# Third feed-forward: second weights centred ahead, squares summed on ScalarE, the up product in three fp32r parts and the bias rows on TensorE

## The chip, the cores and the metric

The kernel runs on one core of one Trainium2 chip. The time is the device time of one execution in microseconds (us). Three runs of the kernel before gave 1136.63, 1144.24 and 1147.08 us (median 1144.24).

The core has a matrix engine (TensorE, PE in the rows, its weight loads PEld), a vector engine (VectorE, DVE), a scalar engine (ScalarE, ACT), a general engine (GpSimd, POOL) and a queue that issues transfers (SyncE, SP).

## The reference, cut to what matters

Eight blocks run one after the other on 2048 tokens of 128 features (attention and feed-forward, four times), each as `x = x + block(layernorm(x))`. The change is in the sixth, the third feed-forward, with eight experts:

```python
def _L2_ffn_ref(x, gate_w, w1, w2, b1, b2, ln_g, ln_b):        # E = 8, D = 128, hidden 256
    scores = xt @ gate_w
    ew, ei = top_k(scores, 2); ew = softmax(ew)
    wE = sum(ew[None] * mask, axis=-1)                          # weight of expert e for token t
    h = gelu(einsum('td,edf->etf', xt, w1) + b1[:, None])
    o = einsum('etf,efd->etd', h, w2) + b2[:, None]
    z = xt[None] + o
    y = (z - mean(z)) * rsqrt(var(z) + 1e-6) * ln_g + ln_b      # over D, for every expert and token
    return einsum('et,etd->td', wE, y)
```

All eight experts are computed for all tokens; the weights of the six that a token does not use are zero. `xt` is itself a layer-normed x, so its mean over D is zero up to rounding.

## The kernel before

Each block is a function that adds instructions to five engine queues; `program` calls them in order, so every engine runs its part of block 5, then of block 6, and so on. Nothing but semaphores ties the queues together. `Norm` normalises x at the start of a block: VectorE writes `xn` (tokens on partitions), TensorE transposes it in four chunks of 512 tokens (`NC` = 4, `CH` = 512, `TPC` = 4 tiles of 128), ScalarE copies each chunk into `xnT`. If a block asks for it (`split_xnT`), ScalarE then also writes each chunk rounded to fp32r (`x_high`), GpSimd the rest of it (`x_low`), and TensorE's `wait_xnT` waits for the second too.

`l2_ffn` (L1309) runs 32 steps, eight experts times four chunks. What a step consists of, engine by engine:

- TensorE: `up` (L1377), two products of 128 x 128 weights with 512 columns in fp32, into two of four banks; `down` of the step before (L1389), eight fp32 products of 128 columns into a bank of its own. One fp32 product stands in the trace as two records.
- ScalarE: two Gelus (L1443) on the results of `up`, into `hT`; then `zn` of three steps before (L1435), four scalings of z by 1/sigma with a shift.
- VectorE: `sums` (L1529) z = result of `down` + (xn + b2); four `bn_stats` (L1533); `shift` of the step before (L1550), -mean/sigma; four `bn_aggr` (L1540) and the variance plus eps (L1543); `add` of three steps before (L1560), four times x += z * weight.
- GpSimd: 1/sigma by a power (L1477); xn + b2 for two steps on (L1466); z * ln_g of two steps before (L1470).
- SyncE: the weights of expert e, 257 KB with b1, into one of two slots (L1339).

The first eight steps are written out, then the engines run a loop over pairs of experts. Ahead of step 0 TensorE computes the router's logits (L1367); it waits until VectorE has copied them (`step`, L1508) before the first `up`. ScalarE takes the router's Exp (L1426) before its first Gelu. In step 0 and 1 the router weights are transposed (L1401) and multiplied with ln_b (L1409), and VectorE adds the four results to x (L1567), in the midst of its first steps.

The next block (`l3_attn`) starts its normalisation on VectorE inside the last steps (`after`, L94 and L98) and has 32 records of TensorE work (L1660) that needs nothing of x.

## Time and profile before

| what | value |
|---|---|
| runs | 1136.63, 1144.24, 1147.08 us |
| profiled execution | 1135.98 us, of which 1134.2 us span |
| busy over the span | PE 917.4 us (81%), DVE 677.8 (60%), POOL 550.0 (48%), ACT 433.0 (38%) |
| mean granted TensorE clock | 0.888 of 2.4 GHz |
| from the first `up` of the block (639.72 us) to the end of the next block's last statistics (796.53 us) | 156.8 us |

In these tables "busy" is the time in which an engine executes; a gap in it costs something only if the engine decides the pace at that place. Rows of the timeline read: start in us, duration in us, engine, line of the kernel, operation, what it writes and reads with partitions x elements, and how many equal ones were merged; in brackets how long the engine had been idle before and what ended that. Groups of instructions read: line, engine, operation, shapes, count, then total busy us and mean ns of one. The granted clock is 1.00 at 2.4 GHz and 0.50 at 1.2 GHz.

### The profile page before, as it was taken

The numbers are of one execution on the slowest core, as the hardware profiler recorded it, in microseconds if no ns is written. First come the engines' busy times: TensorE is split into PE (matmuls) and PEld (weight loads), VectorE is DVE, ScalarE is ACT, GpSimd is POOL, SyncE is SP. The second block draws the span as 40 slices with busy tenths as digits, with TensorE's granted clock in tenths as the row PEclk, the third lists the DMA queues.
The fourth block names the chain that finished last, engine by engine and source line by source line (L and its number), as shares of the span: only waits on it lengthen the run. The fifth ranks groups of instructions, "written<-read, shape, count | busy, mean of one in ns | idle before, by whom it ended". The sixth has DMA issues, their size and how long they took to land. (4 is left out here: it accounts for less than half of the span.)

```text
span 1134.2 us, 18018 instructions
## 1 busy us (share of the span) xinstructions
PE 917.4 (81%) x6494; PEld 592.5 (52%) x6494; DVE 677.8 (60%) x1706; ACT 433.0 (38%) x876; POOL 550.0 (48%) x430
## 2 busy tenths in 40 slices
PE   4559999999989878267999899994699997299993
PEld 2113333333333446164566676663697667199883
DVE  6756667767660255979677479999302475643334
ACT  2334665566555422014111356665344211032221
POOL 4335977897788611152312158888300001146661
PEclk9658999999997988658799699998799998599997
DMA  5700111011000000001000000030200000166665
GB/s 169 222 1 2 29 30 30 2 29 30 3 1 23 1 21 8 9 6 56 2 1 2 1 10 20 19 128 0 75 1 1 1 10 29 55 191 214 211 206 143
DMA packets 37815, 56.40 MB, mean 50 GB/s; under 512 B 5643, under 2 KB 25091, under 8 KB 37607
## 3 DMA queue, kind: packets, MB, share of 16 engines
q1 hardware_dynamic: 35238, 50.21, 14.5%
q0 software_dynamic: 2496, 5.12, 1.6%
q8 instruction: 51, 0.84, 0.3%
q14 instruction: 30, 0.24, 0.1%
HBM read 44.17 MB, written 10.94 MB: 49 GB/s over the span
## 5 line engine op out<-in xcount | busy, mean ns | idle before, releaser
L671 DVE TENSOR_REDUCE arena<-ps 128x2 f32<-128x1024 f32 (+2 forms) x192 | 177.3, 955 | 86.9 <-PE ps L487 55.5
L420 POOL TENSOR_TENSOR arena<-arena 128x1024 f32<-128x1024 f32 (+3 forms) x105 | 201.3, 1957 | 38.8 <-ACT arena L606 38.8
L606 ACT ACTIVATE arena<-ps 128x512 f32<-128x512 f32 (+3 forms) x320 | 138.8, 489 | 91.4 <-PE ps L519 57.6
L117 POOL TENSOR_SCALAR vareps<-meanvar 128x4 f32<-128x4 f32 x32 | 7.8, 245 | 234.6 <-DVE meanvar L98 234.6
L511 PE MATMUL ps<-arena 51*128 51x512 bf16 (+3 forms) x384 | 91.4, 345 | 18.0 <-ACT arena L606 6.8
L152 PE MATMUL ps<-ident,xn 128*128 128x128 f32 x128 | 27.2, 365 | 69.2 <-DVE xn L106 25.4
L511 PEld LDWEIGHTS ps<-arena 51*128 51x128 bf16 x384 | 26.9, 94 | 106.9 <-ACT arena L606 59.7
L2058 PE MATMUL ps<-arena 128*128 128x128 f32 x624 | 78.1, 279 | 0.0
L1389 PEld LDWEIGHTS ps<-arena 128*128 128x128 f32 x512 | 60.8, 192 | 30.7 <-ACT arena L1443 20.3
L2058 PEld LDWEIGHTS ps<-arena 128*128 128x128 f32 x624 | 74.6, 196 | 0.0
L420 POOL TENSOR_TENSOR xnT<-xnT,arena 128x1024 f32<-128x1024 f32 (+1 forms) x28 | 52.8, 1907 | 42.1 <-ACT xnT L606 42.1
L1389 PE MATMUL ps<-arena 128*128 128x128 f32 x512 | 64.6, 279 | 8.4 <-ACT arena L1443 8.4
L487 PE MATMUL ps<-arena 48*128 48x512 bf16 (+3 forms) x320 | 56.1, 346 | 17.5 <-DVE arena L671 14.8
L540 PE MATMUL ps<-arena 128*9 128x512 f32 (+3 forms) x640 | 68.2, 502 | 0.0
L1435 ACT ACTIVATE arena<-arena 128x128 f32<-128x128 f32 x128 | 52.7, 482 | 38.7 <-DVE arena L1550 38.7
L1377 PE MATMUL ps<-xnT,arena 128*128 128x512 f32 x128 | 64.6, 631 | 0.4 <-DVE arena L1508 0.4
L165 ACT ACTIVATE xnT<-ps 128x512 f32<-128x512 f32 x32 | 18.9, 596 | 113.0 <-PE ps L152 106.1
L2224 DVE TENSOR_TENSOR arena<-ps,arena 128x512 f32<-128x512 f32 x39 | 27.0, 691 | 58.5 <-PE ps L2058 57.7
L2018 POOL DMA_INDIRECT expert_rows<-arena x39 | 38.5, 988 | 42.7 <-ACT arena L2106 42.1
L152 PEld LDWEIGHTS ps<-ident,xn 128*128 128x128 f32 x128 | 20.7, 191 | 72.9 <-issue 48.1
L1477 POOL TENSOR_TENSOR arena<-arena,power 128x4 f32<-128x4 f32 x32 | 34.6, 1081 | 46.5 <-DVE arena L1543 46.5
L2005 POOL DMA_INDIRECT arena<-token_rows,arena x39 | 38.0, 974 | 39.0 <-DVEq L2206 27.1
(319 smaller groups left out, 1985.7 us busy)
## 6 DMA issues: line engine op xcount, KB each, us to landing
arena<-in_L_ffn_w SPq DMA_DIRECT2D x39, 512.0 KB, 4.2
arena<-scratch SPq DMA_DIRECT2D x32, 192.0 KB, 3.9
scratch<-arena SPq DMA_DIRECT2D x12, 256.0 KB, 3.9
arena<-in_L_ffn_w SPq DMA_DIRECT2D x8, 257.0 KB, 2.7
arena<-in_L_ffn_w SPq DMA_DIRECT2D x8, 256.0 KB, 4.0
arena<-expert_rows SPq DMA_DIRECT2D x8, 256.0 KB, 4.8
scratch<-arena SPq DMA_DIRECT2D x4, 384.0 KB, 5.1
scratch<-arena SPq DMA_DIRECT2D x12, 128.0 KB, 4.2
```

Of the source, the lines that this page charges most:

```text
L152: last = nc.tensor.transpose(m.ps[:, self.banks[n % len(self.banks)], j * P:(j + 1) * P], m.xn[:, n * TPC + j, :], m.ident[:, :])
L420: nc.gpsimd.tensor_tensor(e, e, weight[:, at:at + k].unsqueeze(1).broadcast_to([P, 2, k]), ALU.mult).then_inc(weighed, 1)
L487: mm = nc.tensor.matmul(m.ps[:, bank + e, 0:wd], qs[rows, u % BUFS, pair, at * P:(at + 1) * P], ks[rows, u % BUFS, pair, j:j + wd], start= ...
L511: mm = nc.tensor.matmul(m.ps[:, bank, 0:wd], ks[rows, u % BUFS, p, kt * P:(kt + 1) * P], qs[rows, u % BUFS, p, CH * qc:CH * qc + wd], star ...
L540: mm = nc.tensor.matmul(m.ps[PAD * h:PAD * h + HD + 1, 7, 0:wd], vones[:, b * TB + kt, u % G * GH + h, :], probs(u * NG + n)[:, h, 0:wd], ...
L606: nc.scalar.activation(probs(g)[:, 2 * p + e, 0:wd], m.ps[:, BANK[h, e], 0:wd], ACT.Exp, scale=SCALE).then_inc(exps, 1)
L671: nc.vector.tensor_reduce(out, scores, AX.X, ALU.max, negate=True).then_inc(max_set, 1)
L1377: mm = nc.tensor.matmul(m.ps[:, 2 * (k % 2) + f, :], w[:, u, W1 + f * P:W1 + (f + 1) * P], m.xnT[:, c * CH:(c + 1) * CH], start=True, stop ...
L1389: mm = nc.tensor.matmul(m.ps[:, 4 + k % 2, j * P:(j + 1) * P], hT[:, k % 2, f, j * P:(j + 1) * P], w[:, u, W2 + f * P:W2 + (f + 1) * P], s ...
L1435: ins = nc.scalar.activation(z[:, k % 4, j, :], z[:, k % 4, j, :], ACT.Identity, bias=nb[:, k % 4, j:j + 1], scale=rs[:, k % 4, j:j + 1])
L2018: nc.gpsimd.indirect_dma_start(m.expert_rows, bass.IndirectOffsetOnAxis(ap=target_i[:, s:s + 1], axis=0), y[:, s % RING, :], None,).then_i ...
L2058: mm = nc.tensor.matmul(m.ps[:, 2 * (s % 2) + half, f * P:(f + 1) * P], w_up[:, s % WBUFS, at + f * P:at + (f + 1) * P], xgT[:, s % 2, :], ...
```

## The change

What it does, in the function `l2_ffn` alone:

- The mean over D is taken out beforehand: w2 has its row means subtracted (`w2_mean` on VectorE, `w2c` on GpSimd, once for each expert), b2 its mean (once). z then has mean zero, so `shift`, `bn_stats` and `bn_aggr` fall away, and so does `zn`. The variance is the mean of z squared: four Square activations with an accumulated output (`squares`) on ScalarE.
- GpSimd computes mean square / D + eps, the power, and its product with the router weight (three small instructions). Its two 128 x 512 instructions in a step fall away.
- b2 enters by TensorE: one fp32r product per step (`pick` selects the two rows, high and low part, of the expert), the first of each `down`.
- `up` becomes three fp32r products for each of its two halves (high x high, high x low, low x high). For that `split_xnT` is asked for, ScalarE rounds w1 (`w1_high`), GpSimd takes the rest (`w1_low`), once for each expert, one expert ahead.
- VectorE: `sums` adds xn directly; `add`, now of two steps before, is y = z * (weight/sigma) * ln_g in four instructions and then x += y in one.
- Order: the first `up` no longer waits for the copied logits; the Exp, the six instructions on the router weights, the transposes and the ln_b products are moved into steps 1, 4, 5 and 6. Loops become written-out steps. z has three buffers instead of four.
- Transfers: b1 for all experts at once, b2 as 2 x 8 rows instead of 512 KB, w without b1 (256 KB), its slots released by the conversions and no longer by `down`.

The diff, cut:

```diff
+    m.rounded.fresh()
+    x_high, x_low = norm.split_xnT()
 ...
+        for e in range(E):
+            if e >= 2:
+                sp.wait_ge(w1_low_set, e - 1)
+                sp.wait_ge(w2_centred, e - 1)
+            sp.dma_start(w[:, e % 2, :], A["L2_ffn_w"][e, :, 0:2 * F]).then_inc(w_in[e % 2], 16)
 ...
+        def up(n):
 ...
+            if n >= 2:
+                pe.wait_ge(h_done, FT * (n - 1))
             for f in range(FT):
-                mm = nc.tensor.matmul(m.ps[:, 2 * (k % 2) + f, :], w[:, u, W1 + f * P:W1 + (f + 1) * P], m.xnT[:, c * CH:(c + 1) * CH],
-                                      start=True, stop=True)
-                mm.then_inc(up_done, 1)
+                nc.tensor.matmul(out, w1_high[:, e % 2, fs], x_high[:, cs], start=True, stop=False)
+                nc.tensor.matmul(out, w1_high[:, e % 2, fs], x_low[:, cs], start=False, stop=False)
+                nc.tensor.matmul(out, w1_low[:, e % 2, fs], x_high[:, cs], start=False, stop=True).then_inc(up_done, 1)
+        def down(n):
 ...
+            if n >= 2:
+                pe.wait_ge(z_done, n - 1)
+            nc.tensor.matmul(m.ps[:, 4 + n % 2, :], pick[:, e, :], b2_rows[:, :].unsqueeze(1).broadcast_to([P, TPC, D]), start=True, stop=False,
+                             skip_group_check=True)
             for f in range(FT):
+                pe.wait_ge(h_done, FT * n + f + 1)
 ...
-        pe.wait_ge(step, 1)
+        for n in range(STEPS):
+            up(n)
+            if n:
+                down(n - 1)
+            if n == 4:
+                turn_weights()
+            if n == 6:
+                norm_biases()
+        down(STEPS - 1)
 ...
+        def squares(n):
+            act.wait_ge(z_done, n + 1)
 ...
+            for j in range(TPC):
+                ins = nc.scalar.activation(square[:, j, :], z[:, n % 3, j, :], ACT.Square, accum_out=ss[:, n % 4, j:j + 1])
 ...
+            if n == 1:
+                act.wait_ge(step, 2 + RANK_STEPS)
+                nc.scalar.activation(gap[:, :], gap[:, :], ACT.Exp).then_inc(exps, 1)
+            if n == 4:
+                for c in range(NC):
+                    turn(c)
+            if n:
+                squares(n - 1)
+            if c == 1 and e + 1 < E:
+                round_weights(e + 1)
 ...
+            nc.gpsimd.tensor_scalar(ve[:, n % 4, :], ss[:, n % 4, :], 1.0 / D, EPS, ALU.mult, ALU.add).then_inc(scales, 1)
+            nc.gpsimd.tensor_tensor(rs[:, n % 4, :], ve[:, n % 4, :], m.power[:, 0:TPC], ALU.pow).then_inc(scales, 1)
+            nc.gpsimd.tensor_tensor(wrs[:, n % 4, :], rs[:, n % 4, :], wte[:, c * TPC:(c + 1) * TPC, e], ALU.mult).then_inc(scales, 1)
+            if c == 1 and e + 1 < E:
+                split_weights(e + 1)
 ...
+        def add(n):
+            e, c = divmod(n, NC)
+            dve.wait_ge(scales, 3 * n + 3)
 ...
             for j in range(TPC):
-                ins = nc.vector.bn_stats(st[:, k % 4, j, :], z[:, k % 4, j, :])
+                ins = nc.vector.scalar_tensor_tensor(out=y[:, j, :], in0=z[:, n % 3, j, :], scalar=wrs[:, n % 4, j:j + 1], in1=lng[:, e, :],
+                                                     op0=ALU.mult, op1=ALU.mult)
 ...
+            nc.vector.tensor_tensor(xs, y[:, :, :], xs, ALU.add).then_inc(y_done, 1)
```

In the lists below a row is one instruction in the order of its engine's queue, or several equal ones in a row (x4); one fp32 matmul is one row here.

VectorE, one step in the midst of the block. Before (L1529 is `sums`, L1533 `bn_stats`, L1550 `shift`, L1540 and L1543 the variance, L1560 `add`):

```order
L1529 TENSOR_TENSOR arena<-ps,arena 128x512
L1533 BN_STATS arena<-arena 128x6 x4
L1550 SCALAR_TENSOR_TENSOR arena<-arena 128x4
L1540 BN_AGGR arena<-arena 128x2 x4
L1543 TENSOR_SCALAR arena<-arena 128x4
L1560 SCALAR_TENSOR_TENSOR x<-arena,x 128x128 x4
```

And of the changed kernel (L1571 is `sums`, L1580 and L1585 are `add`, L1520 and L1522 the mean of w2, once in four steps):

```order
L1571 TENSOR_TENSOR arena<-ps,xn 128x512 [waits l2f_o_done,l2f_y_set]
L1580 SCALAR_TENSOR_TENSOR arena<-arena 128x128 [waits l2f_y_done,l2f_scales]
L1580 SCALAR_TENSOR_TENSOR arena<-arena 128x128 x3
L1585 TENSOR_TENSOR x<-arena,x 128x512 [waits l2f_y_set]
L1520 TENSOR_REDUCE arena<-arena 128x2 [waits l2f_w2_centred,l2f_w_in1]
L1522 TENSOR_SCALAR arena<-arena 128x2 [waits l2f_w2_summed]
```

Of 15 instructions in a step six are left; nothing between `sums` and `add` waits for GpSimd's work on the same step or the one before.

ScalarE, from the last chunk of xnT to step 3, of the changed kernel (L1466 Gelu, L1469 the Exp, L1453 the squares, L1440 the rounding of w1):

```order
L168 ACTIVATE rounded<-xnT 128x512
L1466 ACT_TABLE_LOAD
L1466 ACTIVATE arena<-ps,arena 128x512 x4
L1469 ACT_TABLE_LOAD
L1469 ACTIVATE arena<-arena 128x16
L1453 ACTIVATE arena<-arena 128x128 x4
L1440 ACTIVATE rounded<-arena 128x256
L1466 ACT_TABLE_LOAD
L1466 ACTIVATE arena<-ps,arena 128x512 x2
L1453 ACTIVATE arena<-arena 128x128 x4
```

Before, the same place held one table load:

```order
L165 ACTIVATE xnT<-ps 128x512 x4
L1426 ACTIVATE arena<-arena 128x16
L1443 ACT_TABLE_LOAD
L1443 ACTIVATE arena<-ps,arena 128x512 x4
L1429 ACTIVATE arena<-ps 8x512 x4
```

The Exp has moved behind four Gelus, and the tables are loaded three times in place of once; after that no step loads any.

TensorE, steps 4 and 5 of the changed kernel (L1384 to L1386 are the three parts of `up`, L1397 the bias, L1402 `down`):

```order
L1397 MATMUL ps<-rounded 128x512 [waits l2f_z_done,l2f_w2_centred]
L1402 MATMUL ps<-arena 128x128 [waits l2f_h_done]
L1402 MATMUL ps<-arena 128x128 x3
L1402 MATMUL ps<-arena 128x128 [waits l2f_h_done]
L1402 MATMUL ps<-arena 128x128 x3
L1384 MATMUL ps<-rounded 128x512 [waits l2f_h_done]
L1385 MATMUL ps<-rounded 128x512
L1386 MATMUL ps<-rounded 128x512
```

Where a step had two matmuls of 512 columns and eight of 128, all fp32, it has seven of 512 columns in fp32r and the same eight.

## Rows read from the trace of the kernel before

**Rows 1.** Window, steps 10 to 31: stretch; PE, PEld, DVE, ACT, POOL busy (count); clock; DMA; GB/s.

```profile
697.00:778.00 81.00, 72.79 (x400) 48.89 (x400) 74.41 (x300) 54.77 (x119) 68.76 (x60) 1.00 0.16 55
```

**Rows 2.** Timeline, VectorE, one step and the start of the next.

```profile
749.52 0.69 DVE L1529 TENSOR_TENSOR arena<-ps,arena 128x512 f32<-128x512 f32 x1 [0.19 <-DVE x L1560]
...
750.25 0.87 DVE L1533 BATCH_NORM_STATS2 arena<-arena 128x6 f32<-128x128 f32 x4
...
751.16 0.67 DVE L1550 SCALAR_TENSOR_TENSOR arena<-arena 128x4 f32<-128x4 f32 x1
751.75 0.37 DVE L1540 BATCH_NORM_AGGREGATE arena<-arena 128x2 f32<-128x6 f32 x4
...
752.15 0.17 DVE L1543 TENSOR_SCALAR arena<-arena 128x4 f32<-128x4 f32 x1
752.34 1.14 DVE L1560 SCALAR_TENSOR_TENSOR x<-arena,x 128x128 f32<-128x128 f32 x4
...
753.67 0.69 DVE L1529 TENSOR_TENSOR arena<-ps,arena 128x512 f32<-128x512 f32 x1 [0.19 <-DVE x L1560]
```

**Rows 3.** Timeline, ScalarE and GpSimd, the same step.

```profile
750.54 1.26 POOL L1470 TENSOR_TENSOR arena<-arena 128x512 f32<-128x512 f32 x1
...
751.86 1.65 ACT L1435 ACTIVATE arena<-arena 128x128 f32<-128x128 f32 x4 [1.35 <-DVE arena L1550]
...
752.40 1.17 POOL L1477 TENSOR_TENSOR arena<-arena,power 128x4 f32<-128x4 f32 x1 [0.59 <-DVE arena L1543]
...
753.42 1.24 ACT L1443 ACTIVATE arena<-ps,arena 128x512 f32<-128x512 f32 x2
```

**Rows 4.** Timeline, TensorE, an early step: `up`, `down`, the next `up`.

```profile
664.01 1.88 PE L1377 MATMUL ps<-xnT,arena 128*128 128x512 f32 x4
...
665.73 1.95 PE L1389 MATMUL ps<-arena 128*128 128x128 f32 x16
...
667.51 1.88 PE L1377 MATMUL ps<-xnT,arena 128*128 128x512 f32 x4
```

**Rows 5.** Timeline, TensorE, fp32r products of 512 columns in the next block.

```profile
811.52 0.39 PE L1669 MATMUL ps<-rounded 128*128 128x512 f32 x1
...
811.75 0.39 PE L1670 MATMUL ps<-rounded 128*128 128x512 f32 x1
```

**Rows 6.** Timeline, start of the block: first logits, their copy, `up` of steps 0 and 3.

```profile
630.92 1.81 PE L1367 MATMUL ps<-arena,xnT 128*128 128x8 f32 x8
...
639.38 0.29 DVE L1508 COPY arena<-ps 128x128 f32<-128x128 f32 x1 [7.38 <-PE ps L1367]
...
639.72 6.41 PE L1377 MATMUL ps<-xnT,arena 128*128 128x512 f32 x8 [0.38 <-DVE arena L1508]
...
660.51 1.88 PE L1377 MATMUL ps<-xnT,arena 128*128 128x512 f32 x4
```

**Rows 7.** Timeline, the next block splits a chunk of xnT.

```profile
802.42 0.63 ACT L168 ACTIVATE rounded<-xnT 128x512 fp32r<-128x512 f32 x1
...
803.12 1.40 POOL L125 TENSOR_TENSOR rounded<-xnT,rounded 128x512 fp32r<-128x512 f32 x1 [4.82 <-ACT rounded L168]
```

**Rows 8.** Window, `up` of steps 0 and 1; columns as in rows 1.

```profile
639.70:646.30 6.60, 6.41 (x8) 2.49 (x8) 4.83 (x18) 2.80 (x5) 0.00 (x0) 0.58 0.00 0
```

**Rows 9.** Timeline, ScalarE: the table load ahead of the first Gelu.

```profile
643.70 1.28 ACT L1443 ACT_TABLE_LOAD   x1
```

**Rows 10.** Groups by line and shape: a 128 x 128 Exp, small GpSimd instructions.

```profile
L117 POOL TENSOR_SCALAR vareps<-meanvar 128x4 f32<-128x4 f32 x32 | 7.8, 245 | 234.6 <-DVE meanvar L98 234.6
...
L2100 ACT ACTIVATE arena<-arena 128x128 f32<-128x128 f32 x1 | 0.3, 309 | 0.0
```

**Rows 11.** Timeline, the end: next block's first load, last `down`, last statistics.

```profile
745.24 0.34 SPq L1652 DMA_DIRECT2D arena<-in_L_attn_wqkT  x1
...
775.36 2.02 PE L1389 MATMUL ps<-arena 128*128 128x128 f32 x16 [2.18 <-ACT arena L1443]
...
796.15 0.38 DVE L98 BATCH_NORM_AGGREGATE meanvar<-stats 128x2 f32<-128x6 f32 x4
```

More of the change, by code:

```diff
@@ L1353, in pipelined @@
[L1353 to L1360 removed]
+        sp.dma_start(b1[:, :, :], A["L2_ffn_w"][:, :, B1:B1 + FT].rearrange("e p n -> p e n")).then_inc(small_in, 16)
+        for e in range(E):
[3 more added lines that the diff above has]
+            sp.dma_start(w[:, e % 2, :], A["L2_ffn_w"][e, :, 0:2 * F]).then_inc(w_in[e % 2], 16)
@@ L1376, in up @@
             for f in range(FT):
[L1377 to L1386 removed]
+                fs = slice(f * P, (f + 1) * P)
@@ L1567, in add_biases @@
             nc.vector.tensor_tensor(xs, m.ps[:, 6 + c % 2, :].rearrange("p (j d) -> p j d", d=D), xs, ALU.add).then_inc(lnb_added, 1)
-        def body(i, k, n):
-            sums(i, k, n)
-            if n == 0:
-                for c in range(NC):
-                    add_biases(c)
-                dve.wait_ge(lnb_added, NC)
-            if n is None or n >= 1:
-                shift(i, k - 1)
-            variance(i, k)
-            if n is None or n >= 3:
-                add(i, k - 3, None if n is None else n - 3)
-        def tail():
-            shift(E // 2 - 1, UNROLL - 1, last=True)
-            after(dve, 0)
-            for k in range(UNROLL - 3, UNROLL):
-                add(E // 2 - 1, k, None)
-                after(dve, k % NC)
-        pipelined(dve, body, tail)
-    total = E * NC
-    return Part([(y_done, total - NC + c + 1) for c in range(NC)], tensor=tensor, vector=vector, scalar=scalar, gpsimd=gpsimd, sync=sync,
+        for n in range(STEPS):
+            e, c = divmod(n, NC)
+            sums(n)
+            if n == 1:
+                weights()
+            if n >= 2:
+                add(n - 2)
+                if n - 2 >= STEPS - NC:
+                    after(dve, n - 2 - (STEPS - NC))
+            if n == 5:
+                dve.wait_ge(y_done, n - 1)
+                for k in range(NC):
+                    add_biases(k)
+                dve.wait_ge(lnb_added, NC)
+            if c == 1 and e + 1 < E:
+                sum_weights(e + 1)
+        for n in (STEPS - 2, STEPS - 1):
+            add(n)
+            after(dve, n - (STEPS - NC))
+    return Part([(y_done, STEPS - NC + c + 1) for c in range(NC)], tensor=tensor, vector=vector, scalar=scalar, gpsimd=gpsimd, sync=sync,
                 early=False)
```

267 lines of the change are left out of this document (126 added, 141 removed).

## The prediction

> **What bounds the kernel now.** I read the windows first, then the timeline of one step, then the two ends of the block. In the late part of the block, VectorE is busy for 74.4 of 81.0 us, TensorE for 72.8 and GpSimd for 68.8 [rows 1]; three engines near 90% say little by themselves, so the step decides. VectorE's starts of `sums` lie 4.15 us apart (749.52 and 753.67). Between them it has 0.69 for `sums`, 0.87 `bn_stats`, 0.67 `shift`, 0.37 and 0.17 for the variance, 1.14 `add`, sum 3.91, and 0.19 us of idling that ends with its own `add` [rows 2]. So it waits for no other engine: VectorE sets the pace. One item of it is inflated: `shift` handles 128 x 4 elements and yet takes 0.67 us; it ends at 751.83, when GpSimd's L1470 ends (750.54 + 1.26 = 751.80) [rows 2, 3]. ScalarE waits 1.35 us per step for VectorE and GpSimd 0.59 [rows 3]. TensorE alone is faster: in the early steps, while its lead lasts, `up` to `up` is 667.51 - 664.01 = 3.50 us without a gap, 1.72 for `up` and 1.78 for `down` [rows 4]. The whole block with its tail runs from 639.72 [rows 6] to 796.53 [rows 11].
>
> **TensorE's step after.** An fp32r product of 512 columns starts 0.23 us after the one before (811.52, 811.75) [rows 5]. `up` is six of them, 1.37 us in place of 1.72; `down` keeps 1.75 us (sixteen records, 0.11 each, [rows 4]) and gains one for the bias, 1.98. Sum 3.35 us. That the bias product reads the same 128 columns four times has no row; I take it as the others, and 32 of them at double the price would be 7 us.
>
> **VectorE's step after.** `sums` 0.69; four multiplications at the pace of L1560, 1.14; one sum over 128 x 512, taken as `sums`, 0.69; the mean of w2 once in four steps, at most 0.7, that is 0.17; hand-overs 0.15. Sum 2.85 us in place of 4.1: it is no longer the bound.
>
> **ScalarE's step after.** Two Gelus 1.24 [rows 3], the rounding of w1 at most 0.4 in four steps, 0.1, and four squares. No square with an accumulated output is in the trace. Bound from below: 0.31 us, what a 128 x 128 Exp takes [rows 10]. Above: `zn` has four of the same size in 1.65 us, 0.39 apart, and if the read of the accumulator counts as another 128 x 128 instruction, 0.39 + 0.31 = 0.70. I take 0.35, nearer the Exp, since a square has no per-partition scale and the read hands over one number for each partition. Sum 1.24 + 0.1 + 1.4 = 2.75 us, under TensorE's 3.35; at 0.50 us per square it would reach it.
>
> For the same operation the Trainium skill ("ScalarE: Activation LUTs", What ACT_TABLE_LOAD costs) gives 186 ns plus 0.83 ns per column, 93 ns for each pointer operand, and 93 ns overlap of neighbours. As an estimate from that page a square of 128 columns with one pointer comes to 0.29 us, without the read; the sum would be 2.5 us and the result the same, since TensorE decides.
>
> **GpSimd's step after.** 0.25 [rows 10], 1.06 to 1.17 for the power [rows 3], 0.25, and per expert one instruction of 128 x 256 and two of 128 x 128, each below the 1.26 us of 128 x 512 [rows 3], so under 0.95 per step. At most 2.6 us: hidden. Its chain square, power, weight is needed by `add` two steps later, 6.7 us, and takes about 2; hidden.
>
> **Waits in the loop.** `up(n)` waits for the Gelus of n-2, `down(n)` for the Gelus of n and for `sums(n-2)`. On ScalarE the squares of n-2 stand ahead of the Gelus of n. From the end of `down(n-2)` to `down(n)` TensorE has 1.37 + 1.98 + 1.37 = 4.7 us of work; `sums` 0.9, squares 1.4, Gelu 0.6 and three hand-overs of 0.2 need 3.5. Slack 1.2 us, so no wait is expected: the pace is 3.35 us.
>
> **The block as four stretches, before against after.**
>
> 1. *Start.* TensorE now waits for `x_low` of a chunk before its logits. Behind the transposes ScalarE needs 0.63 us more and GpSimd 1.40 [rows 7], with hand-overs 2.2 us for the first chunk (first logits at 630.92 [rows 6]), and about 1.3 more for the last, whose splitting is only partly hidden. `up(0)` at 643.2 in place of 639.72: **+3.5 us**. VectorE's preparation of the b2 rows and of w2's first mean, thirteen instructions, twelve of them at 0.3 like L1508 and one of 128 x 1024 at twice the 0.69 of 128 x 512, 5 us, lies in its 7.38 us of idling [rows 6].
> 2. *`up(0)` to `up(3)`.* Before 20.8 us (639.72 to 660.51 [rows 6]): transposes and ln_b products lie in it. After: three `up`, two `down`, 8.1 us at full clock; the granted clock was 0.58 in the first 6.6 us, mostly the level of 1.2 GHz [rows 8], and as much time at that level costs 3.3; the second table load and the Exp delay Gelu 2, with about 0.5 us left of it on TensorE. 11.9 us: **-8.9**.
> 3. *`up(3)` to the end of the last `down`* (before 775.36 + 2.02 = 777.38 [rows 11], 116.9 us). After 29 x 1.37 + 30 x 1.98 = 99.1; the transposes, sixteen at 0.11, 1.8 and 0.3 of waiting; the ln_b products, 32 records, 3.5, and 1.5 because their third group waits for VectorE, which adds the first only behind `add(3)`; 0.7 at the last Gelu. 106.9 us: **-10.0**.
> 4. *Tail to the end of the last statistics.* Before 796.53 - 777.38 = 19.2 us, since VectorE was more than one step late. After, VectorE has behind the last `down` `sums` 0.9, three `add` at 1.95 and three statistics at 1.27 (0.87 and 0.38 [rows 2, 11]), hand-overs 0.2 each and a wait for the last scale of some 1: 12.3 us: **-6.9**.
>
> Sum 3.5 - 8.9 - 10.0 - 6.9 = **-22.3 us**, that is 1136.0 - 22 = 1114 against the profiled execution's own time. The next block finds its weights: their transfers began at 745.24 [rows 11], behind the last expert's, and the new release of the slots (by the conversions, one expert earlier) brings them forward. So all that follows moves with it. The three runs before span 1136.6 to 1147.1 and the profiled one is at the lower edge; the middle of that span less 22 is **1119 us**, by the median it would be 1122.
>
> **Table loads.** The Exp's move costs two loads more, 1.28 us each [rows 9], ahead of Gelu 2; after it no step has one. The same page of the Trainium skill counts 2.66 us for a switch, with a drain of 1.38 that no row here shows; by it the two would delay Gelu 2 by 2.8 us more and the sum would be 19.5. The trace decides for the smaller figure: the row holds the 1.28 and no drain.
>
> **Rivals.**
>
> A. *ScalarE becomes the bound.* Above 0.50 us per square each further 0.1 costs 0.4 us per step. At 0.60, the middle of the upper half of my bounds, a step is 3.8 us and the gain falls to 10: 1131 us. For it: no row shows the read. Against it: an Exp with its write of 128 columns takes 0.31. 15%.
>
> B. *VectorE is blocked by GpSimd (slower).* `shift` stood still until L1470 was through [rows 2, 3]. The new `add` reads two SBUF tensors in all five instructions; if each of GpSimd's (some 2.1 us per step with the expert's share) held it up in full, VectorE would need 2.85 + 2.1 = 4.95 us. Thirty-two steps at 4.95 in place of 3.35 are 51 us more than forecast, of which some 10 us fall into waits that stretches 2 to 4 count already: 1119 + 41 = 1160 us. It decides from 1.2 us of blocking per step. Against it: `add` at 752.34 ran beside the power of 752.40 and took 1.14 us for four, no more than at any other place [rows 2, 3], and nearly all of GpSimd's time is now the power. 5%.
>
> The Trainium skill ("SBUF — State Buffer", the part on the shared port pair) says the same as B: a VectorE instruction with two SBUF inputs and a GpSimd instruction that reads SBUF exclude each other for the whole instruction. The stretched `shift` agrees, the unhindered `add` beside the power does not.
>
> C. *The moved pieces cost more than their length.* The router weights pass VectorE, ScalarE's Exp, GpSimd's first scale and TensorE's transposes, and each of them has steps queued behind it. If each hand-over stalls TensorE for a step's length of 3.35 us at two or three places, 8 us are lost: 1127 us. For it: VectorE stands in the ln_b additions, with `sums` behind them. Against: TensorE's lead over `sums` is two steps. 12%.
>
> D. *The fp32r parts run as fp32.* Then `up` is 6 x 0.85 = 5.1 us, a step 7.3 and the time far above 1200. The rows of the next block exclude it but for an unforeseen form [rows 5]. 1%.
>
> **How the numbers follow.** Forecast 65%; A 15, C 12, B 5, D 1, other 2. Range 1104 to 1134: below, the forecast from the lowest run (1136.6 - 22 = 1114.6) with shorter squares, no waits in stretches 2 and 3 and a tail without waiting (some 5 us) and 5 for the scatter of the runs; above, A and C with the same scatter. A difference under 1% (11 us) cannot be told from none here. Faster by over 1%: the forecast, C and two thirds of A, 87%; within 1%: the rest of A and the strong form of C, 7%; slower by over 1%: B and D, 6%.
>
> **What would show it.** Starts of `up` 3.35 us apart with no idle time on TensorE in the late part, at clock 1.00; VectorE some 2.85 us busy per step and waiting for TensorE's `down`; four squares in 1.3 to 1.5 us; `up(0)` 3.5 us later against the first statistics; from the last `down` to the last statistics 12 us. Wrong if squares take over 0.5 us apart, if instructions of `add` end when GpSimd's end, if TensorE waits for a Gelu in each step, or if L1397 takes over 0.25 us.

## The result, and the profile after

| | time, us (median; lowest to highest) | ratio to before, 95% interval |
|---|---|---|
| before | 1144.86 (1136.63 to 1148.09) | |
| after | 1134.14 (1127.27 to 1136.08) | 0.9906, 0.9889 to 0.9922 |
| forecast | 1119 (1104 to 1134) | |

The change gains 10.7 us (0.9%), less than half of what was forecast, and the time lies just outside the range, at its upper end. The profiled execution after spans 1127.3 us; before it was 1134.2.

For all comparisons below I use two marks in the traces, since they leave out the scatter of the other seven blocks: the first transpose of the block (L152) and the end of the last statistics of the next block (L98). Before, they are at 629.08 and 796.53 us, 167.5 us apart. After, 158.3 us apart, and 157.1 in a second profile of the same kernel. The block gained 9 to 10 us, nearly what the medians say (10.7); so nothing of it was given back in the last block. The two profiles of one kernel differ by 1.2 us, nearly all of it ahead of `up(2)`: from the first transpose to `up(2)` it is 21.2 us in one and 20.0 in the other, according to whether the granted clock falls 5 us ahead of the first transpose or only at it. The profiles of the experiments start in one of these two ways (the last two kernels change the start itself), so a difference of about 1 us counts only between two that start alike.

TensorE, the last step of expert 2 and the first of expert 3 after the change (L1384 to L1386 `up`, L1397 the bias product, L1402 `down`; columns as in the timelines of before):

```profile
692.31 0.48 PE L1384 MATMUL ps<-rounded 128*128 128x512 f32 x1
692.63 0.39 PE L1385 MATMUL ps<-rounded 128*128 128x512 f32 x1
...
693.77 0.40 PE L1397 MATMUL ps<-rounded 128*128 128x512 f32 x1
694.01 1.95 PE L1402 MATMUL ps<-arena 128*128 128x128 f32 x16
697.28 0.50 PE L1384 MATMUL ps<-rounded 128*128 128x512 f32 x1 [1.33 <-POOL rounded L1484]
...
700.71 0.48 PE L1384 MATMUL ps<-rounded 128*128 128x512 f32 x1
```

This answers to [rows 4]. Inside an expert `up` follows `up` after 3.40 us, as at 697.28 and 700.71, without a gap. But from the last step of one expert to the first of the next it takes 4.97 us (692.31 to 697.28): TensorE waits for L1484, GpSimd's part of the splitting of w1. An expert takes 15.20 us (697.28, 712.48, 727.68, 742.88, 758.08) where four steps are 13.6. The view of the waits of TensorE between 641 and 775 us (us in total, times, longest):

```profile
PE ps L1384 <- POOL rounded L1484: 8.5, 6, 1.9
PE ps L1422 <- DVE x L1590: 1.4, 1, 1.4
PE ps L1412 <- ACT arena L1458: 0.2, 1, 0.2
```

Why the split is late stands in two more timelines of the same stretch. ScalarE (L1440 rounds w1, L1453 the squares of step 9):

```profile
691.17 0.40 ACT L1440 ACTIVATE rounded<-arena 128x256 fp32r<-128x256 f32 x1
...
693.38 0.31 ACT L1453 ACTIVATE arena<-arena 128x128 f32<-128x128 f32 x1 [0.66 <-DVE arena L1571]
693.60 0.19 ACT L1453 ACTIVATION_READ_ACCUMULATOR arena<-arena 128x1 f32 x1
693.70 0.29 ACT L1453 ACTIVATE arena<-arena 128x128 f32<-128x128 f32 x1
```

GpSimd (L1498 to L1504 the three scale instructions of a step, L1484 the split, L1489 the centring of w2):

```profile
692.95 0.21 POOL L1504 TENSOR_TENSOR arena<-arena 128x4 f32<-128x4 f32 x1
694.83 0.35 POOL L1498 TENSOR_SCALAR arena<-arena 128x4 f32<-128x4 f32 x1 [1.67 <-ACT arena L1453]
695.26 1.01 POOL L1500 TENSOR_TENSOR arena<-arena,power 128x4 f32<-128x4 f32 x1
696.35 0.20 POOL L1504 TENSOR_TENSOR arena<-arena 128x4 f32<-128x4 f32 x1
696.50 0.73 POOL L1484 TENSOR_TENSOR rounded<-arena,rounded 128x256 fp32r<-128x256 f32 x1
697.21 1.28 POOL L1489 TENSOR_SCALAR arena<-arena 128x128 f32<-128x128 f32 x2
```

The rounded w1 of expert 3 is there at 691.57. GpSimd is free from 693.16 to 694.83, but the split stands in its queue behind the scales of step 9, and these wait for the squares of step 9, which end at 694.7. The split is over at 697.23; TensorE could have started at 695.7. "One expert ahead" in the code is, in time, not ahead at all: when GpSimd works on step 9, TensorE, which leads by two to three steps, is already at the end of step 11.

The second place is behind step 6, where the ln_b products now lie (L1422). Timeline of TensorE after the change, from the end of step 6 to `up` of step 8:

```profile
668.23 1.95 PE L1402 MATMUL ps<-arena 128*128 128x128 f32 x16
670.11 2.05 PE L1422 MATMUL ps<-arena 8*128 8x128 f32 x16
673.53 3.22 PE L1422 MATMUL ps<-arena 8*128 8x128 f32 x16 [1.38 <-DVE x L1590]
676.68 0.80 PE L1384 MATMUL ps<-rounded 128*128 128x512 f32 x1
677.28 0.63 PE L1385 MATMUL ps<-rounded 128*128 128x512 f32 x1
...
679.84 2.50 PE L1402 MATMUL ps<-arena 128*128 128x128 f32 x16
682.10 0.48 PE L1384 MATMUL ps<-rounded 128*128 128x512 f32 x1
```

And the window of the last 5.3 us of it (stretch; PE, PEld, DVE, ACT, POOL busy; clock; DMA; GB/s):

```profile
676.70:682.00 5.30, 5.30 (x23) 4.62 (x23) 1.28 (x3) 1.37 (x2) 1.20 (x2) 0.59 0.20 49
```

The forecast had the products and the wait, 5.0 us; they take 6.6 (670.11 to 676.68). It did not have the clock: in the second half of the products it falls to 1.2 GHz, the products take twice as long, and nearly all of the next step is slow too, 5.42 us in place of 3.40 (676.68 to 682.10).

### The profile page after: what moved, and what is told of

The parts are those of the page before. It is cut to its first block and busy times, and to the rows that moved or that the text cites. A ratio compares the mean times of both kernels' runs of the same rounds, so it can differ in the third digit from the quotient of the medians.

```text
span 1127.3 us, 17905 instructions
## 1 busy us (share of the span) xinstructions
PE 908.3 (81%) x6590; PEld 612.6 (54%) x6590; DVE 646.1 (57%) x1445; ACT 429.1 (38%) x1018; POOL 510.8 (45%) x458
## 5 line engine op out<-in xcount | busy, mean ns | idle before, releaser
L152 PE MATMUL ps<-ident,xn 128*128 128x128 f32 x128 | 26.4, 356 | 62.1 <-DVE x L922 19.9
L2076 PEld LDWEIGHTS ps<-arena 128*128 128x128 f32 x624 | 74.7, 196 | 0.0
L2242 DVE TENSOR_TENSOR arena<-ps,arena 128x512 f32<-128x512 f32 x39 | 27.0, 692 | 66.0 <-PE ps L2076 34.7
L1402 PEld LDWEIGHTS ps<-arena 128*128 128x128 f32 x512 | 63.0, 194 | 2.9
L1402 PE MATMUL ps<-arena 128*128 128x128 f32 x512 | 62.9, 276 | 0.0
L152 PEld LDWEIGHTS ps<-ident,xn 128*128 128x128 f32 x128 | 20.0, 186 | 66.0 <-issue 40.7
L1453 ACT ACTIVATE arena<-arena 128x128 f32<-128x128 f32 x128 | 38.0, 298 | 35.8 <-DVE arena L1571 35.8
L1267 DVE TENSOR_TENSOR arena<-ps,arena 128x512 f32<-128x512 f32 x64 | 39.7, 682 | 17.6 <-PE ps L1149 17.6
L2110 ACT ACTIVATE arena<-ps 128x512 f32<-128x512 f32 x39 | 23.3, 597 | 68.1 <-PE ps L2076 58.3
```

The source lines that it names most:

```text
L152: last = nc.tensor.transpose(m.ps[:, self.banks[n % len(self.banks)], j * P:(j + 1) * P], m.xn[:, n * TPC + j, :], m.ident[:, :])
L1267: nc.vector.tensor_tensor(at[:, t % 2, g, :].rearrange("p (j q) -> p j q", q=P), m.ps[:, g, :].rearrange("p (j q) -> p j q", q=P), causal[ ...
L1402: mm = nc.tensor.matmul(m.ps[:, 4 + n % 2, j * P:(j + 1) * P], hT[:, n % 2, f, j * P:(j + 1) * P], w2c[:, e % 2, f, :], start=False, stop= ...
L2076: mm = nc.tensor.matmul(m.ps[:, 2 * (s % 2) + half, f * P:(f + 1) * P], w_up[:, s % WBUFS, at + f * P:at + (f + 1) * P], xgT[:, s % 2, :], ...
```

## The experiments

Each kernel was timed against the kernel before, in the same session. "Block" is the time between the two marks, from the profile of that kernel; "expert" is TensorE's time for the four steps of an expert in the late part.

| kernel | ratio, 95% interval | block, us | expert, us |
|---|---|---|---|
| the changed kernel again | 0.9909, 0.9880 to 0.9939 | 157.1 | 15.20 |
| e1, split early on both engines | 0.9835, 0.9799 to 0.9870 | 148.0 | 13.60 |
| e11, only GpSimd's order | 0.9820, 0.9771 to 0.9869 | 149.8 | 13.60 |
| e2, `up` in fp32 | 0.9913, 0.9880 to 0.9947 | 156.1 | 14.95 |
| e3, no ln_b part | 0.9802, 0.9766 to 0.9838 | 147.8 | 15.20 |
| e4, e1 without b2 | 0.9752, 0.9724 to 0.9780 | 141.0 | 12.69 |
| e5, e1, ln_b in two halves | 0.9790, 0.9753 to 0.9828 | 144.2 | 13.60 |
| e6, e1, ln_b in four pieces | 0.9800, 0.9766 to 0.9833 | 143.4 | 13.60 |
| e7, e1, ln_b padded to 128 rows | 0.9839, 0.9802 to 0.9877 | 144.8 | 13.60 |
| e8, e5 and e7 together | 0.9787, 0.9759 to 0.9814 | 141.8 | 13.60 |
| e9, e6 and products in the waits at the start | 0.9797, 0.9760 to 0.9834 | 141.8 | 13.60 |
| e10, e8 and more of these | 0.9730, 0.9677 to 0.9783 | 138.8 | 13.60 |

The kernels without the ln_b part (e3) and without b2 (e4) leave out a part of the output; all others compute the whole. The intervals are 3 to 6 us wide to each side; smaller differences between these kernels are read from the block, of which there is one profile for each kernel. From the first transpose to `up(2)` the changed kernel, e11 and e7 have 21.2 us, and e4 21.0, being without the bias product; the changed kernel again, e1, e3, e5, e6 and e8 have 20.0 to 20.1. So 1.1 us has to be taken off the block of e4, e7 or e11 before it is compared with that of e1.

**Is the missing gain in the waits for the split?** The reference for the others first.

> The changed kernel as it stands, for the scatter of its runs and as the partner of the runs beside it. Both theories expect about 1134 us and 0.991 of the kernel before, as measured; on TensorE six waits for the split of w1 (L1484) of 8.5 us in all, of them five of 1.33 us at the first step of experts 3 to 7, 15.20 us per expert, and the step from 673.5 to 682.1 us at the lower clock.

As expected: six waits of 8.5 us, 15.20 us per expert. The first experiment moves the rounding and the split of w1:

```diff
 # ScalarE, step n
+            if n % NC == 0 and e + 1 < E:
+                round_weights(e + 1)
             if n:
                 squares(n - 1)
-            if c == 1 and e + 1 < E:
-                round_weights(e + 1)
 # GpSimd, step n; split_weights cut in two: split_w1 and centre_w2
+            if c == 0 and e + 1 < E:
+                split_w1(e + 1)
...
             if c == 1 and e + 1 < E:
-                split_weights(e + 1)
+                centre_w2(e + 1)
```

> Only the order changes: ScalarE rounds w1 of expert e+1 in step 4e ahead of its squares (was step 4e+1 behind them), and GpSimd splits it ahead of the scales of step 4e (was behind those of 4e+1). Theory W (the missing gain stands in TensorE's waits for the split): those waits vanish, an expert takes 4 x 3.40 = 13.6 us in place of 15.2, the time falls by 8.5 us to about 1126, 0.983 of the kernel before. Rival S (TensorE waits for what its followers do, and another of them is just as late: Gelu, sums or squares): the wait has another name, an expert stays at 14.8 to 15.2 us and the time within 2 us of the changed kernel, 0.990. Rival N (the block is shorter, the time is not, because the last block takes it back): an expert takes 13.6 us and the time is still 1132 or more.

Theory W holds: no wait for L1484 is left on TensorE, every expert takes 13.60 us, the time is 9.2 us below the changed kernel's in the same session (1116.09 and 1125.24), the block 9.1 us shorter. Rivals S and N fall. The waits had cost 10.0 us of pace; 1.0 of it is lost again at the ln_b products, where `up(6)` to `up(8)` takes 16.57 us in place of 15.52. The window from 697 to 757 us of the changed kernel (columns as above):

```profile
697.00:757.00 60.00, 55.50 (x368) 49.93 (x368) 42.44 (x104) 40.78 (x164) 33.15 (x59) 1.00 0.20 70
```

And of e1:

```profile
697.00:757.00 60.00, 60.00 (x409) 54.76 (x408) 46.78 (x114) 43.75 (x178) 38.77 (x66) 1.00 0.20 70
```

TensorE goes from 55.5 to 60.0 us busy; VectorE with 46.8 and ScalarE with 43.8 follow.

e1 moved work on two engines. Whether the place in one queue is enough:

```diff
 # GpSimd, step n, ahead of its three scales; ScalarE as in the change
+            if c == 1 and e + 1 < E:
+                split_w1(e + 1)
...
             if c == 1 and e + 1 < E:
-                split_weights(e + 1)
+                centre_w2(e + 1)
```

> The smallest edit: on GpSimd alone the split of w1 for expert e+1 stands ahead of the three scale instructions of step 4e+1 in place of behind them; ScalarE's rounding stays where the change put it. Theory Q (the place in GpSimd's queue alone is the cause: in the changed kernel w1_high of expert 3 is there at 690.8 us, GpSimd idles from 692.38 to 694.05, and the split runs at 695.73, because the scales of step 9 wait ahead of it): the split runs 3.3 us earlier, 3 us before TensorE wants it, all six waits vanish, an expert takes 13.6 us, and the time is that of e1_split_early, 0.983 of the kernel before. Rival R (ScalarE's rounding is late as well): waits of 0.5 us or more remain and the gain is below 5 us.

Theory Q holds, R falls. GpSimd's timeline in this kernel (L1503 to L1509 are the scales here):

```profile
698.88 0.20 POOL L1509 TENSOR_TENSOR arena<-arena 128x4 f32<-128x4 f32 x1
699.03 0.74 POOL L1484 TENSOR_TENSOR rounded<-arena,rounded 128x256 fp32r<-128x256 f32 x1
700.75 0.73 POOL L1503 TENSOR_SCALAR arena<-arena 128x4 f32<-128x4 f32 x1 [0.98 <-DVE arena L1585]
```

And TensorE's first `up` of expert 3 in it, with no wait ahead of it:

```profile
701.64 0.48 PE L1384 MATMUL ps<-rounded 128*128 128x512 f32 x1
```

The split now ends at 699.77, 1.9 us before TensorE wants it. One block of code three instructions further up is worth 8.5 us (149.8 us for the block here, 158.3 in the profile of the changed kernel that starts like it; against the other, 157.1, it would be 7.3).

**What was the three-part product worth?** `up` as one fp32 product again, without the splitting of x and w1; all else as changed:

```diff
-                nc.tensor.matmul(out, w1_high[:, e % 2, fs], x_high[:, cs], start=True, stop=False)
-                nc.tensor.matmul(out, w1_high[:, e % 2, fs], x_low[:, cs], start=False, stop=False)
-                nc.tensor.matmul(out, w1_low[:, e % 2, fs], x_high[:, cs], start=False, stop=True).then_inc(up_done, 1)
+                nc.tensor.matmul(out, w[:, e % 2, W1 + f * P:W1 + (f + 1) * P], m.xnT[:, cs], start=True, stop=True).then_inc(up_done, 1)
```

> Undoes one part of the change: up is one fp32 product for each half, as before, and w1 and x are not split; all else stays. Theory W (in the changed kernel the gain of the three-part product, 0.35 us per step, went into the waits for the split of w1): a step is 1.72 + 0.23 + 1.75 and 0.05 = 3.75 us with no wait between experts, 15.0 us per expert against 15.2, the start is 3 us earlier, and the time is 3 us below the changed kernel, 0.988 of the kernel before. Rival V (the changed kernel is held by another engine's step and the waits only follow from it): an expert still takes over 15.2 us and the time is above the changed kernel's.

One step on TensorE in this kernel (L1383 `up`, L1394 the bias, L1399 `down`):

```profile
706.42 1.88 PE L1383 MATMUL ps<-xnT,arena 128*128 128x512 f32 x4
707.74 0.80 PE L1394 MATMUL ps<-rounded 128*128 128x512 f32 x1
708.38 1.95 PE L1399 MATMUL ps<-arena 128*128 128x128 f32 x16
710.16 1.02 PE L1383 MATMUL ps<-xnT,arena 128*128 128x512 f32 x2
```

A step is 3.74 us (706.42 to 710.16), an expert 14.95, with no wait between experts: V falls. The block is 1.0 us shorter than the changed kernel's, not 3: the start is 3.2 us earlier (10.0 us from the first transpose to `up(0)`, 13.2 there), but the first three steps take 1.2 us more, and the step behind the ln_b products, at the lower clock, 2.0 us more (6.81 and 4.82). The ratio is that of the changed kernel. So in the change as made the three-part product brings nothing that these runs can tell from none; with the split early it is worth 8 us of the block (156.1 and 148.0).

**Is TensorE's own work the pace once the split is early?** e1 without the bias product is a test of it; the first product of `down` then opens the bank (its `start` flag, not in this cut).

```diff
-            nc.tensor.matmul(m.ps[:, 4 + n % 2, :], pick[:, e, :], b2_rows[:, :].unsqueeze(1).broadcast_to([P, TPC, D]), start=True, stop=False,
-                             skip_group_check=True)
```

> The early split of e1_split_early; leaves b2 out of the output: no bias product at the head of down. Theory T (with the split early TensorE's own work sets the pace and nothing else): a step takes 0.23 us less, 3.17 us, an expert 12.7 us, and the time is 7.3 us below e1_split_early, 0.977. Rival S (VectorE, ScalarE or GpSimd stand close behind): a new wait appears on TensorE, an expert stays at 13.2 us or more and the time falls by less than 4 us.

An expert takes 12.69 us and the block is 7.0 us shorter, 7.8 from `up(3)` to the end of the last `down` (T said 7.3): T holds, S falls. VectorE, busy for 45.2 of 53 us (697 to 750 us), is not reached even then. The bias product costs its 0.23 us in every step, although it reads the same 128 columns four times.

**What do the moved ln_b pieces cost?** All of them left out, with what belongs to them on ScalarE and VectorE:

```diff
-            if n == 4:
-                turn_weights()
-            if n == 6:
-                norm_biases()
```

> Leaves out the ln_b part of the output: the transposes of the router weights (L1412), their copies (L1458), the 16 ln_b products (L1422) and the four additions (L1590). Theory M (the moved pieces cost their length, the wait for VectorE and a stretch at the lower clock): 2.1 + 6.6 us and 2.7 us for the step at the lower clock go, and 1.3 us of waiting for the split appears at step 8, net -10 us, about 1124 us, 0.982. Rival L (the clock falls for another reason and the pieces cost only their length): -1.8 - 3.5 - 1.4 + 1.3 = -5.4 us, about 1129 us, 0.986. The waits for L1484 stay.

The block is 9.2 us shorter; M gave 10, L 5.4. A seventh wait for L1484 appears, at step 8, where TensorE had been too late to wait. So the ln_b part costs 9 us net, of which only 5.3 are its instructions on TensorE (1.8 and 3.5 in the forecast). The next experiments, on e1, ask what makes the clock fall: the wait in the midst of the products, or the products themselves.

```diff
-            if n == 6:
-                norm_biases()
+            if n in (6, 7):
+                norm_biases((2 * n - 12, 2 * n - 11))
 # VectorE
-            if n == 5:
+            if n in (5, 6):
                 dve.wait_ge(y_done, n - 1)
-                for k in range(NC):
+                for k in (2 * n - 10, 2 * n - 9):
                     add_biases(k)
```

> The early split of e1_split_early, and the ln_b products in two halves, two chunks behind step 6 and two behind step 7, with VectorE's additions behind its steps 5 and 6, so that the third chunk finds its bank free. Theory M: the wait of 1.4 us goes, and with it the stretch at the lower clock (2.7 us): 4 us less than e1_split_early, about 1122 us, 0.980. Rival K (the clock falls because of what the ln_b products are, eight rows of weights, not because of the wait): only 1.4 us less, about 1124.5 us, and the step behind the second half is at the lower clock again.

TensorE in this kernel, from the second half of the products to `up` of step 9:

```profile
672.45 2.05 PE L1422 MATMUL ps<-arena 8*128 8x128 f32 x16
674.43 0.50 PE L1384 MATMUL ps<-rounded 128*128 128x512 f32 x1
...
675.69 0.51 PE L1386 MATMUL ps<-rounded 128*128 128x512 f32 x1
676.00 0.63 PE L1397 MATMUL ps<-rounded 128*128 128x512 f32 x1
676.43 3.29 PE L1402 MATMUL ps<-arena 128*128 128x128 f32 x16
679.47 0.48 PE L1384 MATMUL ps<-rounded 128*128 128x512 f32 x1
```

The size is M's (the block is 3.8 us shorter than e1's), the mechanism is not: no wait is left, TensorE is busy all the time, and still the clock falls at 675.8 (0.51 from there to 679.3), behind the second group of products with eight rows of weights (`8*128`), and the step there takes 5.04 us. That is K's mechanism. K's size was too small because the products themselves are all at the higher clock now, 2.05 us; in e1 the last sixteen took 3.78:

```profile
671.60 3.78 PE L1422 MATMUL ps<-arena 8*128 8x128 f32 x16 [1.37 <-DVE x L1595]
```

> The early split, and the ln_b products in one block as in e1_split_early, but ln_b and the turned router weights padded with zeros to 128 rows, so that each product reads 128 rows of weights in place of eight; the products are as long. Theory K (the rows make the clock fall): the clock stays at 1.00 from the products to the next step, up of step 7 to up of step 8 takes 3.4 us in place of 5.9, and the time is 4 us below e1_split_early. Rival W (the 1.4 us of waiting between the two halves make it fall): 0.50 in this stretch as before, and the time of e1_split_early.

TensorE in this kernel, the 32 records, the next step and its successor:

```profile
665.43 1.95 PE L1424 MATMUL ps<-arena 128*128 128x128 f32 x16
668.95 2.05 PE L1424 MATMUL ps<-arena 128*128 128x128 f32 x16 [1.57 <-DVE x L1602]
670.76 0.48 PE L1385 MATMUL ps<-rounded 128*128 128x512 f32 x1
...
674.17 0.48 PE L1385 MATMUL ps<-rounded 128*128 128x512 f32 x1
```

Its window over the products:

```profile
665.00:671.00 6.00, 4.43 (x39) 4.24 (x38) 4.41 (x9) 1.73 (x9) 2.78 (x5) 1.00 0.00 0
```

This settles it between the two: 32 records that last as long and have an even longer wait between them (1.57 us), but with 128 rows in place of eight (120 of them zeros), and the clock stays at 1.00; the next step takes 3.41 us. The eight rows made the clock fall here, not the wait. Both operands of these products have eight rows (`8*128` and `8x128`) and both were padded, so it stays open which of them counts. The block is 3.2 us shorter than e1's, 4.3 with the later start of this profile taken off (`up(6)` to `up(8)` is 12.22 us in place of 16.57), where K said 4; the ratio of the times, 0.9839, does not show it within its interval.

> The early split, and the ln_b products in four pieces behind steps 6 to 9, one chunk each, with VectorE's additions behind its steps 5 to 8. In e5_lnb_halves the clock still fell behind the second half (675.8 to 679.3 us). Theory K (it falls when many of the products with eight rows of weights lie close together): it does not fall, and the time is 1.6 us below e5_lnb_halves, less 0.3 for two more interruptions: 2.7 us below e1_split_early x 1 + 2 more, that is 5 us below it, 0.979 at the most. Rival H (it falls at this place for another reason): one step of some 5 us at the lower clock is there as in e5_lnb_halves, and the time is that of e5_lnb_halves.

Four pieces between full steps keep the clock at 1.00 too; each piece costs 1.29 us, the price of an interruption and its eight records. That is K again. The block is 0.8 us shorter than with halves; the times are equal within their intervals.

> The early split, ln_b and the turned router weights padded to 128 rows as in e7_lnb_wide, and the ln_b products in two halves as in e5_lnb_halves. If the effects add (the wait of 1.6 us goes by the halves, the lower clock by the padding), the block from its first transpose to the end of the last down is 133.1 - 1.6 + 0.2 = 131.7 us, the same as e6_lnb_quarters (131.7), and the time is about 0.979 of the kernel before. If the halves and the padding remove the same thing, it is 133 us.

The effects add: the block takes 141.8 us, and from the first transpose to the end of the last `down` it is 130.1. The 131.7 that was expected started from e7's 133.1, which has 1.1 us of later start in it; without that it would have been 130.6.

**The low clock at the start.** Before and after, the first steps run for the most part at 0.50 ([rows 8]; after, 0.61 from 641.0 to 648.5). e9 and e10 put fp32 products of the identity with itself, into a bank that is free, into TensorE's waits; e9 has three, e10 six:

```diff
+        spin(2)
         for t in range(NT):
             if t % TPC == 0:
-                norm.wait_xnT(pe, t // TPC)
+                norm.wait_xnT(pe, t // TPC, lambda: spin([1, 0, 2, 1][t // TPC]))
```

> e6_lnb_quarters with three products of 512 columns whose results are not used, two in the 3.2 us in which TensorE waits ahead of the block's first transpose, one in the 1.5 us ahead of the first logits. Theory F (the logits and the first three ups run at 1.2 GHz because TensorE idles before them): the clock is at 1.00 by the logits, the last x_low comes 2 us earlier because the third and fourth transposes do, the first three ups take 1.4 instead of 2.6 us each, and the time is 5 us below e6_lnb_quarters, 0.976. Rival G (the logits, with eight columns, and the waits between them hold the clock down): 0.50 until up(1) as before, the first transpose 0.2 us later, and the time is that of e6_lnb_quarters, 0.980.

Neither theory holds as stated. The clock is 1.00 from 627 to 633 us and 0.52 from 633 to 643; the block is 1.6 us shorter than e6's, 2.7 if one allows for the clock having fallen 5 us ahead of the block here, as in the changed kernel, and not in e6. The fall is at 633.3, within the transposes of the third chunk, and so ahead of TensorE's wait of 1.7 us for the third `x_low` (634.10 to 635.79), not in it, as the next expectation has it.

> e8_halves_wide with products whose results are not used in TensorE's waits at the start of the block: two ahead of the first transpose, one ahead of the first logits, and, new against e9_warm (there the clock fell at 633.9 us, in the wait for the third x_low), two ahead of the third chunk's logits and one ahead of the fourth's. Theory F (the clock falls where TensorE waits at the start): 1.00 from the first transpose to the first three ups, 1.4 us each in place of 2.6, the block from the first transpose to the end of the last down 125 to 127 us in place of 130.1, and the time 0.975. Rival G (the logits, with eight columns of output, hold it down whatever lies between): 0.50 again from the third logits to up(1), 128.5 us as e9_warm gained, 0.978.

TensorE in this kernel, the last logits with the unused products (L1371) and the first two `up` (L1392):

```profile
643.66 1.03 PE L1379 MATMUL ps<-arena,xnT 128*128 128x8 f32 x8 [0.29 <-POOL rounded L125]
644.55 1.10 PE L1371 MATMUL ps<-ident 128*128 128x512 f32 x2
645.49 0.95 PE L1379 MATMUL ps<-arena,xnT 128*128 128x8 f32 x8
646.30 0.48 PE L1392 MATMUL ps<-rounded 128*128 128x512 f32 x1
...
647.77 0.40 PE L1392 MATMUL ps<-rounded 128*128 128x512 f32 x1
```

This is theory F: 1.00 throughout, `up` takes 1.4 us from the first on, and it is 127.1 us from the first transpose to the end of the last `down`. That the six products together hold the clock is seen against e8, where it falls at the first transpose. That the three added since e9 do it is not shown: up to the third chunk's transposes both kernels give TensorE the same work, and the clock fell there in e9, where it had already been at 0.50 ahead of the block, and not in e10, where it had not.

`up(0)` comes 2.3 us earlier than in e8 and `up(2)` another 2.0 us, but the block gains only 3.0. The rest stands in a new wait, for the Gelu (L1476) of step 2:

```profile
657.39 2.05 PE L1410 MATMUL ps<-arena 128*128 128x128 f32 x16 [0.97 <-ACT arena L1476]
```

ScalarE has its third table load ahead of this Gelu, from 655.36 to 656.64. So the Exp between the Gelus does cost TensorE about 1 us, once the first steps run at the higher clock.

The ratio is 0.973 (0.968 to 0.978), 31 us less than before on the median before of 1144.86 and some 20 us less than the change: this version beats both.

## Why the prediction was wrong, point by point

The stretches of the prediction, the first one counted from the first transpose:

| stretch | forecast | measured |
|---|---|---|
| 1, start | +3.5 | +3.1 (10.64 to 13.75 us) |
| 2, `up(0)` to `up(3)` | 11.9 us, -8.9 | 10.8 us, -10.0 |
| 3, `up(3)` to the end of the last `down` | 106.9 us, -10.0 | 122.0 us, +5.1 |
| 4, tail | 12.3 us, -6.9 | 11.7 us, -7.5 |
| sum | -22.3 | -9.2 |

**The step that failed is "GpSimd's step after ... At most 2.6 us: hidden."** It weighed GpSimd's load and never asked at which place of its queue the split of w1 stands, what that place waits for, and when TensorE wants the result. The list of "Waits in the loop" has the Gelu and the sums, and not w1_low, although `up` waits for it in every fourth step. In stretch 3 this cost 2.1 us at step 4 and five times 1.6, some 10 in all (8.5 of waiting, and 0.2 more each time until the pace is regained). e11, with that place alone changed, is 8.5 us shorter: 0.2 is left at step 4, and 1.4 is lost again at the ln_b products. It could have been seen from the order and the prediction's own durations: the squares of step 4e+1 follow two steps behind TensorE, GpSimd's scales come behind them, then the split.

**The second miss is the clock behind the ln_b products**: 2.0 us in the step behind them, and 1.2 us in the products' second half (3.22 in place of 2.05), most of the 1.75 us by which they, with their wait, lengthened the step beyond the 5.0 (10.15 us from `up` to `up`, less 3.40). The trace of before held the sign. In its timeline of TensorE the `up` behind the last ln_b products takes 3.58 us instead of 1.88:

```profile
655.21 3.58 PE L1377 MATMUL ps<-xnT,arena 128*128 128x512 f32 x4
```

I read it as part of the slow start. The rest of the 15.1 us of stretch 3 is the pace, 3.40 us in place of 3.35 (1.5 us over 29 steps), less 0.3 us elsewhere: the six products of `up` take 1.46 us to the bias product, not 1.37 (692.31 to 693.77; the first is followed by the second only after 0.32), and `down` 1.70, not 1.75. With both causes removed, in e7, the same stretch takes 108.5 us (649.56 to 758.04), the forecast of 106.9 and the pace. In e8 it takes 106.6 (646.60 to 753.24); that this is the forecast almost to the tenth is luck, since e8 is also without the wait between the products, for which the forecast had 1.5.

**What held.** TensorE as the bound inside an expert, and the fp32r and bias products at 0.23 us. Four squares take 1.19 us up to the next instruction (693.38 to 694.57): each is an ACTIVATE of 0.29 us and a record of its own for the read of the accumulator, 0.19 us, half of which lies under the next square, so that squares start 0.29 us apart. Forecast 1.4, so rival A falls. VectorE's step: `sums` 0.69, `add` 1.13 and 0.69. The tail, against [rows 11], is 11.7 us; it begins with the end of this row of TensorE:

```profile
772.02 1.95 PE L1402 MATMUL ps<-arena 128*128 128x128 f32 x16
```

and ends with this one of VectorE:

```profile
785.28 0.38 DVE L98 BATCH_NORM_AGGREGATE meanvar<-stats 128x2 f32<-128x6 f32 x4
```

Rival B falls as a bound (it would have decided from 0.5 us of blocking per step, 3.35 less 2.85, and not from the 1.2 that it names). But something like its mechanism is seen beside the split of w1 and the centring of w2, once per expert, in VectorE's timeline after the change:

```profile
696.67 1.72 DVE L1580 SCALAR_TENSOR_TENSOR arena<-arena 128x128 f32<-128x128 f32 x4
```

These four run beside the split (from 696.50 above) and end at 698.39, the centring (from 697.21) at 698.49; elsewhere four take 1.13 us, and in e11, beside the split alone, 1.51. VectorE has the room. The rule of the Trainium skill that the prediction named for B ("SBUF — State Buffer", the part on the shared port pair) agrees with this row. Whether it holds for the power as well stays open: [rows 2, 3] speak against it, and after the change the two no longer lie side by side in a usual step (`add` from 693.27 to 695.12, the power from 695.26). In one step of e11 they do for 0.35 us (the power from 705.31 to 706.35, `add` from 706.00), and both take what they take alone, 1.04 and 1.13 us.

The numbers of rivals A and C, 1131 and 1127 us, are nearer to the 1134 measured than the forecast is, but neither mechanism was at work. C looked at the router weights, whose transposes wait 0.2 us, and at the ln_b additions, which were in the sum with 1.5 and cost 1.4, and not at w1; that the moved ln_b pieces cost more than their length is true, but by the clock. No rival had a conversion that is late once per expert.

In the change as made the Exp between the Gelus made no wait on TensorE, for which the forecast had 0.5 us: stretch 2 was 1.1 us shorter than forecast. That rests on the slow first steps; at the higher clock, in e10, the wait is there with 0.97 us. No drain is seen in either: in e10 the last square's read ends at 655.34, the load runs from 655.36 to 656.64 and the Gelu starts at 656.65.

Two sums of the prediction are slightly off without bearing on it: the middle of the three runs before, 1141.9, less 22 is 1120 and not 1119, and rival D's step is 5.1 + 1.98 = 7.1 us and not 7.3.

## What to carry to other kernels

A helper engine with half its time free can still hold up the leader: for every tile that it hands on, write down the instruction ahead of it in its queue, what that one waits for, and how many steps the leader is in front. "One expert ahead" counts from the helper's place in the program, not from the leader's. When a faster form of an operation needs such a preparation (here the split for the three-part product), its gain is only there once the preparation is early; try it against the plain form. And if a gain of TensorE is sought, look at its granted clock behind products over few rows; here padding them to 128 rows with zeros made no product longer and kept the clock.

## What the runs showed of the hardware that I had not expected

The granted clock fell to 1.2 GHz while TensorE was busy without a gap: after two groups of sixteen records with eight rows (e5, 675.8 us). It fell too, with a wait between the groups, in the changed kernel and in e1, e2, e4 and e11. The same records padded to 128 rows left it at 2.4 GHz, even with 1.57 us of idling between them (e7), and in groups of eight records between full steps they left it there without padding (e6). The Trainium skill ("TensorE: Matmul & The Clock Gate", Part 1: The HAM clock gate) describes the clock as following how busy the engine has recently been; the start of this block agrees (waits filled with unused products gave 1.00 where it had been 0.50, e10), the ln_b products do not, since the engine was busy there in the sense of the profile.

At the start, six unused products, put where TensorE waited, were worth about 3 us of the block (141.8 to 138.8, one profile each).
